# One transformer layer on one core: the order of the second half, and where four of sixteen score steps are masked

## The reference

```python
x = L0_attn_x                                   # (16, 512, 256)
x = _layernorm(x + attention(x))
x = _layernorm(x + ffn(x))
# attention: 16 heads of 16, a window of the 128 tokens before each query (dist > 0, dist <= 128)
scores = where(allowed, q @ k^T / 4, NEG);  local = softmax(scores) @ v
# and a latent path: 64 pooled tokens, 4 heads of 16, whose result is `remote`
gate = sigmoid(local @ gl_w + remote @ gr_w)
out  = (gate * local + (1 - gate) * remote) @ out_w + out_b
# ffn: two ternary linear layers with an rms norm ahead of each, and an exact gelu between them
```

## Time and profile before

| what | value |
|---|---|
| median of three runs | 1172.93 us (1171.77 to 1175.84) |
| the profiled execution | 1171.74 us, span of its instructions 1170.0 us |
| busy: PE / PEld / DVE / ACT / POOL | 994.1 / 634.8 / 823.3 / 741.7 / 628.1 us |
| prologue, to the first S step | 98.0 us |
| one sequence in the middle | about 66.4 us: first half 21.6, second half 44.9 |

### The profile page before, as it was taken

How to read it: one execution, slowest core, us unless ns; L and a number is a source line. 1 busy time by engine, 2 the same in 40 slices (tenths; PEclk the granted TensorE clock), 3 DMA queues, 4 the chain that set the end, 5 groups by cost and what they waited for, 6 DMA issues and landing times. The chain is left out here.

```text
span 1170.0 us, 37047 instructions
## 1 busy us (share of the span) xinstructions
PE 994.1 (85%) x15432; PEld 634.8 (54%) x15432; DVE 823.3 (70%) x1781; ACT 741.7 (63%) x1189; POOL 628.1 (54%) x790
## 2 busy tenths in 40 slices
PE   6765999898989989888999889898989988884755
PEld 3444565565656555565656555565656555562433
DVE  4485777786868777686868778686867768684544
ACT  3523666767676676767676677767676676762544
POOL 6014455665746465664746466574745466572754
PEclk8896999999999999999999999999999999996887
DMA  5731331506152341516143240516143250601000
GB/s 192 199 103 57 109 92 48 152 24 182 40 154 66 100 120 48 137 40 181 40 127 93 86 133 28 157 40 180 40 128 92 68 135 10 176 21 38 1 19 19
DMA packets 58868, 107.46 MB, mean 92 GB/s; under 512 B 20518, under 2 KB 38726, under 8 KB 55622
## 3 DMA queue, kind: packets, MB, share of 16 engines
q1 hardware_dynamic: 58556, 105.08, 31.8%
q10 hardware_dynamic: 144, 0.00, 0.0%
HBM read 70.87 MB, written 33.55 MB: 89 GB/s over the span
## 5 line engine op out<-in xcount | busy, mean ns | idle before, releaser
L847 ACT ACTIVATE Pt<-scores 128x1024 f32<-128x1024 f32 (+1 forms) x256 | 229.6, 917 | 143.9 <-PE oacc L1552 82.0
L1125 DVE TENSOR_REDUCE nmax<-work 128x3 f32<-128x480 f32 x352 | 215.1, 633 | 31.5 <-PE work L1503 28.2
L701 POOL TENSOR_TENSOR h_lo<-hbuf,h_hi 128x512 f16<-128x512 f32 x128 | 148.1, 1157 | 139.8 <-DVE h_hi L1252 139.8
L671 POOL TENSOR_SCALAR_AFFINE_SELECT Pt<-Pt 128x512 f32<-128x512 f32 x256 | 164.2, 642 | 67.6 <-ACT Pt L847 67.2
L685 POOL TENSOR_TENSOR rs<-rs,power 128x6 f32<-128x6 f32 x32 | 42.4, 1325 | 247.5 <-DVE rs L1229 247.5
L1552 PE MATMUL oacc<-Pt,Vp 128*32 128x256 f32 (+1 forms) x2048 | 153.2, 360 | 15.2 <-POOL Pt L675 9.4
L1529 PE MATMUL scores<-Qs,Ks 100*32 100x160 bf16 (+4 forms) x4096 | 119.9, 230 | 46.9 <-DMA Qs<-nmax_pair 25.7
L1498 PE MATMUL work<-Ks,Qs 98*32 98x160 bf16 x4096 | 146.3, 236 | 14.5 <-DVE nmax L1125 10.5
L1252 DVE CAST h_hi<-hbuf 128x512 f16<-128x512 f32 x128 | 69.2, 540 | 100.3 <-ACT hbuf L883 99.8
L1529 PEld LDWEIGHTS scores<-Qs,Ks 100*32 100x32 bf16 x4096 | 82.4, 98 | 92.2 <-ACT Pt L847 51.0
L1382 PE MATMUL scores<-xT,wqk 128*128 128x512 f32 x256 | 123.3, 616 | 6.5 <-DMA xT<-x_t 6.5
(11 more groups left out here) (175 smaller groups left out, 1878.5 us busy)
## 6 DMA issues: line engine op xcount, KB each, us to landing
parts_scratch<-parts SPq DMA_DIRECT2D x96, 256.0 KB, 5.1
Qs<-parts_scratch SPq DMA_DIRECT2D x96, 256.0 KB, 5.0
Ks<-parts_scratch SPq DMA_DIRECT2D x96, 256.0 KB, 5.0
xT<-x_t SPq DMA_DIRECT2D x16, 512.0 KB, 4.0
xres<-x SPq DMA_DIRECT2D x16, 512.0 KB, 4.8
y<-nat SPq DMA_DIRECT2D x16, 512.0 KB, 3.0
Qs<-nmax_pair SPq DMA_DIRECT2D x256, 2.0 KB, 1.8
nat<-up_t SPq DMA_DIRECT2D x1, 1024.0 KB, 6.0
```

The source lines that it names most:

```text
L671: ins = pool.affine_select(out=pt[:, :, 0:P], in_=pt[:, :, 0:P], compare_op=ALU.is_gt, fill=0.0, base=0, pattern=[[0, 4], [1, P]], channel ...
L701: pool.tensor_tensor(h_lo[:, t % NR, :], hbuf[:, t % 2, :], h_hi[:, t % NR, :], ALU.subtract).then_inc(h_lo_ready, 1)
L847: nc.scalar.activation(Pt[:, u % NPT, :, 0:w], scores[:, slot, :, :].rearrange("p k (h q) -> p (k h) q", h=2)[:, :, 0:w], ACT.Exp, scale=S ...
L1125: nc.vector.tensor_reduce(nmax[:, first:first + n], work[:, slot, 0:n * BAND].rearrange("p (h c) -> p h c", h=n), X, ALU.max, negate=True) ...
```

## The change

- `SECOND_HALF` is rewritten. The output products stand behind the third query-key product; the fourth follows the second output product. The norm steps and the transposes stand earlier; `VALUES`+0 stands ahead of `LAT_RKV`, `SPLIT`+7 behind it, and `LAT_SCORES` behind `VALUES`+1. `LAT_EXP` and `LAT_EXP`+1 stand behind `XN_HI` and `XN_LO`. From `VALUES`+2 on the list is as before.
- `XN_LO`: VectorE subtracts the fp16 part from the bank and writes the rest. Before, TensorE subtracted it in the bank with a matmul and ScalarE copied it out.
- Score steps 1, 5, 9 and 13: TensorE writes a mask of 0 and -1e30 into the bank with four matmuls of 256 columns, and the score matmuls add to it. GpSimd does nothing for these steps, and PV waits for ScalarE instead.
- `move_max`: 8 DMAs to a scratch tensor in DRAM, a wait for them, and one DMA of 32 KB from there into both rows. Before, 16 DMAs went directly.
- The prologue: P steps of sequence 1 stand between the A steps of sequence 0, not ahead of them, and `LAT_O` of sequence 0 stands ahead of both.

```diff
 SECOND_HALF = (
     ("F", GATE), ("P", QK), ("P", QK + 1), ("P", SPLIT), ("P", QK + 2), ("P", SPLIT + 1), ("P", SPLIT + 2),
-    ("P", QK + 3), ("P", SPLIT + 3), ("F", OUT), ("P", SPLIT + 4), ("P", SPLIT + 6), ("P", LAT_RQ), ("P", SPLIT + 5),
-    ("F", OUT + 1), ("P", SPLIT + 7), ("P", LAT_RKV), ("P", VALUES), ("P", LAT_SCORES), ("F", NORM),
-    ("F", NORM + 1), ("P", LAT_EXP), ("P", VALUES + 1), ("F", XN_T), ("F", XN_T + 1), ("F", XN_HI),
-    ("P", LAT_EXP + 1), ("F", XN_LO), ("P", VALUES + 2), ("F", UP), ("P", LAT_NORM), ("F", UP + 1),
+    ("F", OUT), ("P", SPLIT + 3), ("P", SPLIT + 4), ("F", OUT + 1), ("P", QK + 3), ("P", SPLIT + 5), ("F", NORM),
+    ("P", LAT_RQ), ("P", SPLIT + 6), ("F", NORM + 1), ("P", VALUES), ("P", LAT_RKV), ("P", SPLIT + 7),
+    ("F", XN_T), ("F", XN_T + 1), ("P", VALUES + 1), ("P", LAT_SCORES), ("F", XN_HI), ("F", XN_LO), ("P", LAT_EXP),
+    ("P", LAT_EXP + 1), ("P", VALUES + 2), ("F", UP), ("P", LAT_NORM), ("F", UP + 1),
...
+BY_PE = (1, 5, 9, 13)
+BY_POOL = tuple(u for u in range(NU) if u not in BY_PE)
...
-    order += [("P", 1, k) for k in split]
-    order += [("P", 0, LAT_O), ("P", 1, LAT_RQ), ("P", 1, LAT_RKV), ("W", 0, SUMS)]
...
+    order.append(("P", 0, LAT_O))
+    after = {0: [(0, REMOTE), (1, QK)], 1: [(1, QK + 1), (1, SPLIT)], 2: [(0, REMOTE + 1)],
+             3: [(1, QK + 2), (1, SPLIT + 1), (1, SPLIT + 2)], 4: [(1, QK + 3), (1, SPLIT + 3)],
+             5: [(1, SPLIT + 4), (1, SPLIT + 6)], 6: [(1, SPLIT + 5), (1, LAT_RQ), (1, SPLIT + 7)], 7: [(1, LAT_RKV)],
...
             def move_max(s):
...
+                for g in range(NG):
+                    for j in range(2):
+                        sp.dma_start(scratch[g, :, j], nmax_pair[g * GT:(g + 1) * GT, j, :].rearrange(
+                            "p (k w) -> p k w", k=2)).then_inc(nmax_out, 16)
+                wait_alone(sp, nmax_out, count(s, 1, 0) * 16 * 2 * NG)
+                sp.dma_start(Qs[s.par][MAXR:MAXR + 2, :, :].rearrange("j h n -> j (h n)"), nmax_dram
+                             ).then_inc(nmax_in[s.par], 16)
...
+                if k == XN_LO:
+                    for t in range(KT):
+                        dve.wait_ge(xn_hi, count(s, KT, t))
+                        nc.vector.tensor_tensor(xnT[:, 1, t, :], oacc[:, t, :], xnT[:, 0, t, :], ALU.subtract
+                                                ).then_inc(xn_lo, 1)
...
+                if u in BY_PE:
+                    for c in range(4):
+                        nc.tensor.matmul(scores[:, slot, c // 2, (c % 2) * 2 * P:(c % 2) * 2 * P + w], identb[:, :],
+                                         key_mask[:, 0:w], start=(c % 2 == 0), stop=False, skip_group_check=True)
```

More of the change, by code:

```diff
@@ L142, in order_of_prologue @@
     order += [("P", 0, LAT_T), ("P", 0, LAT_T + 1), ("W", 0, CONSTANTS)]
-    order += [("P", 1, k) for k in split]
-    order += [("P", 0, LAT_O), ("P", 1, LAT_RQ), ("P", 1, LAT_RKV), ("W", 0, SUMS)]
[L145 to L149, removed]
+    order.append(("P", 0, LAT_O))
+    after = {0: [(0, REMOTE), (1, QK)], 1: [(1, QK + 1), (1, SPLIT)], 2: [(0, REMOTE + 1)],
+             3: [(1, QK + 2), (1, SPLIT + 1), (1, SPLIT + 2)], 4: [(1, QK + 3), (1, SPLIT + 3)],
+             5: [(1, SPLIT + 4), (1, SPLIT + 6)], 6: [(1, SPLIT + 5), (1, LAT_RQ), (1, SPLIT + 7)], 7: [(1, LAT_RKV)],
+             8: [(1, VALUES)], 9: [(1, LAT_SCORES)], 11: [(1, LAT_EXP)], 12: [(1, LAT_EXP + 1), (1, VALUES + 1)],
+             14: [(1, LAT_NORM), (1, LAT_NORM + 1)], 15: [(1, VALUES + 2)], 17: [(1, LAT_T), (1, LAT_T + 1)],
+             18: [(1, VALUES + 3)], 19: [(1, LAT_O)], 21: [(1, REMOTE), (1, REMOTE + 1)]}
+    between = {v: [("P", i, k) for i, k in steps] for v, steps in after.items()}
+    between[13] = [("W", 0, SUMS)]
     for v in range(NM):
@@ L537, in move_max @@
                 wait_alone(sp, nmax_split, count(s, 1, 0))
[L538 to L545, removed]
+                if not s.first:
+                    wait_alone(sp, nmax_in[1 - s.par], (s.half + s.par) * 16)
+                scratch = nmax_dram.rearrange("j (k r g w) -> g r j k w", k=2, g=NG, w=GT)
+                for g in range(NG):
[5 more added lines that the diff above has]
+                             ).then_inc(nmax_in[s.par], 16)
             def store_before(s):
@@ L740, in body @@
                 for u in range(NU):
-                    mask(s, u)
+                    if u in BY_POOL:
+                        mask(s, u)
                     if u == STAT_AT + NB and not s.first:
@@ L1532, in scores_T @@
                             kk[0:KB, key + lo:key + lo + GT],
-                            q[0:KB, place, j * P + lo:j * P + hi], start=True, stop=True)
+                            q[0:KB, place, j * P + lo:j * P + hi], start=(u not in BY_PE), stop=True,
+                            skip_group_check=True)
                 mm.then_inc(s_full[slot], 1)
@@ L1595, in f_step @@
                                 mm.then_inc(xn_T, 1)
-                if k == XN_LO:
-                    for t in range(KT):
-                        pe.wait_ge(xn_hi, count(s, KT, t))
-                        nc.tensor.matmul(oacc[:, t, :], minus[:, :], xnT[:, 0, t, :], start=False, stop=True,
-                                         skip_group_check=True).then_inc(xn_rest, 1)
                 if k == UP:
```

25 lines of the change are left out of this document (15 added, 10 removed).

## The result

The changed kernel takes 1223.54 us (median of four runs, 1217.25 to 1225.81), the kernel before 1172.48 in the same series. The ratio is 1.0421, with a 95% interval of 1.0377 to 1.0465. That is inside the forecast range (1174 to 1234), on the side forecast, and 13.5 us above the forecast of 1210. Three executions in the experiments (one of run B, one of run F and one of the kernel before beside them), at a mean granted clock of 0.65 to 0.74 instead of about 0.96 and over 10% longer than the others, are left out, and as the one of run B is its profiled one, no stage is read from that run.

What follows compares the result with a forecast made beforehand. Bound: the relay through ScalarE to the second half's first GELU, with TensorE full only at the end. Sum: 1171.74 + 36.4 + 11 - 6 - 2 - 2.2 + 2 - 1.4 = 1209.5, so 1210 us; range 1174 to 1234.

Steps and rivals of the forecast that it cites:

- The relay: Second half, ScalarE's queue up to the first GELU: GELU 2.6 us later in 14 sequences, +36.4 us.
- The table load, the sign to look for: Second half, ScalarE: table load at about +26.3 us from the half's start, 23.7 before, if the forecast is right.
- The stands: Second half, TensorE idle: 2.3 us ahead of VALUES+1, some 3 us ahead of UP+2 until the first GELU.
- sequences 14 and 15: Second halves without P steps: XN_LO on VectorE runs beside UP's first part, -0.7 us each, -1.4.
- The clock: TensorE behind the longer stand: one half-clock stretch per sequence, 0.8 us x 14 = +11; bounds none and +48.
- The first half: Masks of four score steps moved from GpSimd to TensorE: -0.4 us in each of 15 first halves, -6.
- its bound for a loss: First half: a loss up to 1.0 us if PE, near 20.5 of 21.7 us busy, now decides.
- TensorE bounds the first half: Rival: masks cost 1.0 us each, +15 more, 1225 us; no separate chance, 0.06 for results above 1234 together.
- The sign given for the mask term: First half: GpSimd (POOL) busy 13 us and the half's length within 1 us, if the mask forecast is right.
- sequence 15, forecast at -2: First half of sequence 15, no A steps, so GpSimd counts there: -2 us from the masks.
- The new way: Maxima by way of DRAM (move_max): saves 2.4 us in the prologue and 2.2 for sequence 15, hidden in 14 sequences.
- The interleaving: Prologue, sequence 1's P steps between sequence 0's A steps: +4.2 us, +2 after the 2.4 saved on maxima.

Runs made afterwards that it cites:

- run B: experiment 1 with all sixteen score steps masked by GpSimd; 1151.61 us, 0.9831 of the kernel before.
- run F: The kernel before with XN_LO subtracted by VectorE and the maxima moved by way of DRAM; 1145.68 us, ratio 0.9785.
- experiment 1: The changed kernel with the SECOND_HALF list of the kernel before, all else kept; 1156.42 us, 0.991 of the kernel before.
- experiment 2: The changed kernel with SPLIT+7 moved ahead of LAT_RKV; 1194.12 us, 1.0221 of the kernel before.
- experiment 9: experiment 8 with NORM moved ahead of SPLIT+7 and NORM+1 ahead of LAT_SCORES; 1185.25 us, 1.0111 of the kernel before.
- run E: The kernel before with XN_LO subtracted by VectorE as the only edit; 1154.51 us, ratio 0.987.
- experiment 4: The filler: the changed kernel with XN_T transposes and VALUES+3 products computed three times over where TensorE stands; 1210.69 us, 1.0371 of the kernel before.
- experiment 8: run F with OUT moved ahead of the fourth query-key product and OUT+1 behind SPLIT+4; 1154.44 us, 0.9868 of the kernel before.
- run D: The changed kernel with the 16 direct DMAs of before for the maxima; 1230.37 us, 1.0527 of the kernel before.

## Why the prediction was right, and where it was not

**The relay: right, almost to the tenth.** Put on the changed kernel's clock (+23.03), the forecast times and the rows are: fourth product's copy on ScalarE 558.8 and 558.92; end of the last split copy 565.4 and 565.41; `VALUES`+1 565.4 and 565.51; VectorE done with the shifts 571.4 and 571.58; GELU 573.7 and 573.84. The table load, the sign to look for, starts 26.4 us behind the half's start, forecast 26.3. The stands were forecast at 2.3 and 3, and are 2.00 and 2.63. The delay where no low clock precedes it is 26.85 less 24.14 = 2.7, forecast 2.6, and nothing of it is given back behind the GELU (20.52 and 20.61). Experiments 1 and 2 show by edits that it is the order on ScalarE's queue, the bank included, and experiment 9 the same on another list.

**What the forecast did not see in it.** Its 2.6 us is a difference of two effects. The list costs 4.3 a half (experiment 1 against the changed kernel), 3.7 of it order and 0.6 clock; `XN_LO` on VectorE gains 1.0 (run E). The forecast named the copies and matmuls that `XN_LO` saves, but took them into the end of the relay and gave them a price of their own only in sequences 14 and 15. The sum was right; it does not say that one part of the change is good by itself.

**The clock: near in size, wrong in place.** One stretch of 3.4 us at half clock for each middle sequence, two in four of them and one of 6.8 us in sequence 12; 0.8 a half was forecast, 0.6 measured by experiment 4, 8.7 us for 11. But the forecast put the stretch behind the longer stand and charged it there. Where it lies there alone it costs nothing (47.38 against 47.37 with the filler) or 0.1 (experiment 2: 20.65 from the GELU to the end, 20.51 with the filler); the cost comes from those behind the first, shorter stand. That the size is near is partly luck. The clock fell behind stands of 2 to 2.6 us, though not behind every one (the first stand, 2.00 us, in 10 halves of 14), and it did not fall with waits up to 0.94, nor with the 1.40 of experiment 8. The Trainium skill's page "TensorE: Matmul & The Clock Gate" (What's actually happening), by which activity is what releases the throttle, agrees with experiment 4, where repeated matmuls alone keep the row at full speed.

**The first half: the step that failed.** "I take -0.4 (the last select lies on the path to the last product)" measured +0.6 in the changed kernel, +0.5 with the masks alone. Over 13 first halves this is 13.0 of the 14.7 us by which the sum by stages was short. The cost of the masked steps was not the mistake (2.7 us a half measured, 2.6 at most forecast), but that TensorE would take them in. The forecast had the numbers for it: PE near 20.5 of 21.7 by its own sum, 20.60 of 21.81 measured, and its bound for a loss. It took GpSimd's end of the path because that was visible at the last product, and counted the other 15 steps as if an engine at 94% had room. The rival "TensorE bounds the first half" is what happened in this part, but its 1225 is near the measured 1223.5 by chance: it took 1.0 us a half, where 0.6 was measured, and added 15 to a sum that has -6 in it, so that by its own figures it should have said 1231. The sign given for the mask term (POOL 13 us, the length within 1 us) came true, since it was too wide to tell -0.4 from +0.6. In sequence 15, forecast at -2 because GpSimd would count there, GpSimd's busy time fell from 16.76 to 12.21 us and the first half still grew from 21.08 to 21.99; TensorE is busy only 15.55 us of it, so it isn't full there, and what holds this half I did not isolate.

**`move_max` and the prologue: two errors that cancel.** The new way was forecast to save 2.4 and 2.2; it saves 3.3 in the prologue and 3.9 in sequence 14. An issue to DRAM takes 3.61 / 8 = 0.45 us, not the 0.63 of the rows; the last DMA, taken as 2.4, took 101.80 less 98.58 = 3.2. The Trainium skill's page "DMA: Bandwidth & Descriptors" (Why small descriptors are slow (HBM only)) warns of small pieces to DRAM; no penalty shows in the landing here, each of the eight lands in about 1.5 us where the direct ones took 1.8. The fixed cost of 2.0 us, which the forecast took from the same page of the Trainium skill (Anatomy of one DMA), is given there for DMAs on the path through GpSimd, and SP issues these; the eight stay below it, the last one is above. The forecast's chain of 8.8 us comes to 8.7 when it is added up again, which changes nothing. The interleaving was forecast at +4.2 and costs 6.9. In the profiled execution the A stage starts 0.6 us later than forecast (49.09), TensorE works 36.9 us in it for a forecast 36.2, and 4.3 us of gaps stay for a forecast 3.0. Up to the gate of sequence 0 the two gave +1.9 for a forecast +1.6. In the profiled executions the new way also shortens the first half of sequence 0 by about 2 us (27.74 in run D, 25.30 in the changed kernel; 26.92 in run E, 24.76 in run F); by what path I did not isolate.

**The parts by ratio:** list +60 us, `XN_LO` -15, masks +7, prologue +7, maxima -5 (traces) to -12 (ratios): 47 to 54 against 51 measured.

## What to carry to other kernels

When engines walk one list, read off the chain of the resource whose late arrival nothing gives back (here the fourth product, its splits, the `lat_bd` copies, the exponentials, the table load, the GELU) and ask of every entry that is moved whether it now stands ahead of a link on any queue. "Earlier" for the output products was "5 us later" for the fourth product (its first copy on ScalarE 12.8 us behind the half's start instead of 7.8), and a norm copy moved into what looked like idle time cost its full length. An engine that a move brings to 94% of a stage had no room for the work of another at 81%, even where the last wait of the stage is on the second. And take a change apart on the chip before judging it: a 4% loss held a 2% gain.

## What the runs showed of the hardware

- Stands of TensorE of 2 to 2.6 us were followed by 3.4 us at half clock; two such stands a sequence mostly gave one such stretch, not two. A stretch in front of the GELU cost up to 1.4 us, one behind it next to nothing in most halves. Filling the stands with repeated matmuls took 8.7 us off the fourteen second halves (experiment 4).
- The direct DMAs of 2 KB between SBUF partitions cost SP 0.63 us an issue, the ones of 4 KB to DRAM 0.45.
- Two subtractions from PSUM to fp16, 128x512, took VectorE 1.29 us, 0.69 each and 0.6 from start to start; the shape was not in the trace of before, and the nearest rows gave its length.
- A block of four full-array matmuls among 32-column tiles takes TensorE 0.54 us where the four by themselves are 0.45, and the block ahead of it 0.57 instead of 0.43: an estimated 0.2 for going from one tile shape to the other and back, as had been allowed for.
